# Recurrence, first sequence: rounding the weights and taking their residuals two heads ahead, at the end of a step

## What is computed

```python
q = silu(causal_dwconv(xn @ Wq, qconv_w, qconv_b))     # 4 taps along the tokens
k = silu(causal_dwconv(xn @ Wk, kconv_w, kconv_b))
q, k = layernorm over each head's 128 channels, with weight and bias
v = xn @ Wv
beta = sigmoid(xn @ Wb + bb)
def step(S, inp):                                       # one token, per sequence and head
    S = (1.0 - b) * S + b * (v_t[..., :, None] * k_t[..., None, :])
    o_t = jnp.einsum('bhvk,bhk->bhv', S, q_t)
o = o * silu(xn @ Wg);  return o @ Wo
```

## Time and profile before

| what | value |
|---|---|
| the profiled execution | 2600.33 us, span 2598.5 us |
| median of three runs | 2605.1 us |
| PE busy over the span | 2456.1 us (95%) |
| DVE, ACT, POOL busy | 1904.5, 1241.8, 849.1 us |
| mean granted clock of PE | 0.977 of full speed |
| recurrence | about 100 to 1815 us of the span |
| its first sequence | about 100 to 550 us |

### The profile page before, as it was taken

The page is one execution under the profiler, slowest core; times in us unless marked ns, Lnnn a source line. Parts: engine busy times, 40 slices in busy tenths (PEclk is TensorE's granted clock), DMA queues, the critical chain, the costliest instruction groups (busy, mean ns, idle before and its releaser), DMA issues. The chain is left out here.

```text
span 2598.5 us, 43686 instructions
## 1 busy us (share of the span) xinstructions
PE 2456.1 (95%) x14784; PEld 2175.3 (84%) x14784; DVE 1904.5 (73%) x3396; ACT 1241.8 (48%) x2025; POOL 849.1 (33%) x442
## 2 busy tenths in 40 slices
PE   4889989989999999999999999996999998999997
PEld 4778878889999989999989999996788887888886
DVE  5589999989999999999999999998422123432232
ACT  5455455545555656555555555554533223322221
POOL 1245544433434343443434343444000000221220
PEclk9999999999999999999999999998999999999999
DMA  7566566576655675666676656664551102431320
GB/s 283 166 212 212 194 221 221 201 263 205 215 195 211 210 274 195 211 218 205 210 249 231 200 204 210 211 208 142 180 204 49 65 32 73 151 121 45 113 90 23
DMA packets 242375, 462.74 MB, mean 178 GB/s; under 512 B 59382, under 2 KB 162038, under 8 KB 221178
## 3 DMA queue, kind: packets, MB, share of 16 engines
q10 hardware_dynamic: 107648, 244.34, 27.3%
q1 hardware_dynamic: 125946, 192.21, 22.0%
q0 software_dynamic: 8704, 25.19, 3.1%
HBM read 371.99 MB, written 98.07 MB: 181 GB/s over the span
## 5 line engine op out<-in xcount | busy, mean ns | idle before, releaser
L1023 DVE SCALAR_TENSOR_TENSOR xn_rows<-ps_proj,conv,xn_rows 128x1021 f32<-128x1021 f32 x381 | 486.8, 1278 | 11.6 <-ACT xn_rows L900 2.5
L1221 PE MATMUL ps_proj<-xt_hi,w_hi 128*128 128x512 f32 x1008 | 409.0, 406 | 20.1 <-DMA xt_lo<-scratch_xt_lo 12.0
L1223 PE MATMUL ps_proj<-xt_hi,w_lo 128*128 128x512 f32 x1008 | 398.5, 395 | 0.0
L1222 PE MATMUL ps_proj<-xt_lo,w_hi 128*128 128x512 f32 x1008 | 397.1, 394 | 0.0
L784 POOL TENSOR_TENSOR rc_k_state<-rc_tok_k,k_norm_rows 128x1024 f32<-128x1024 f32 x64 | 153.6, 2400 | 599.6 <-DVE rc_q_silu L1035 511.9
L1243 PE MATMUL ps_proj<-wv_hi,xt_hi 128*128 128x256 f32 x1024 | 295.2, 288 | 0.7 <-PEq L75 0.7
L1244 PE MATMUL ps_proj<-wv_lo,xt_hi 128*128 128x256 f32 x1024 | 289.8, 283 | 0.0
L1245 PE MATMUL ps_proj<-wv_hi,xt_lo 128*128 128x256 f32 x1024 | 289.8, 283 | 0.0
L1221 PEld LDWEIGHTS ps_proj<-xt_hi,w_hi 128*128 128x128 f32 x1008 | 191.9, 190 | 59.1 <-DMA xt_lo<-scratch_xt_lo 13.3
L1653 DVE TENSOR_TENSOR ff_wide_lo<-ff_wide,ff_wide_hi 128x512 fp32r<-128x512 f32 x64 | 44.4, 693 | 248.7 <-ACT ff_wide_hi L1568 248.7
L1223 PEld LDWEIGHTS ps_proj<-xt_hi,w_lo 128*128 128x128 f32 x1008 | 191.4, 190 | 42.0
(11 more groups left out here) (181 smaller groups left out, 5757.0 us busy)
## 6 DMA issues: line engine op xcount, KB each, us to landing
rc_q_rows<-scratch_rows ACTq DMA_DIRECT2D x64, 1024.0 KB, 5.1
rc_k_rows<-scratch_rows ACTq DMA_DIRECT2D x64, 1024.0 KB, 4.6
rc_decay_all<-scratch_decay ACTq DMA_DIRECT2D x64, 512.0 KB, 5.4
rc_cum_all<-scratch_cum ACTq DMA_DIRECT2D x64, 512.0 KB, 3.7
scratch_o<-rc_o_sb ACTq DMA_DIRECT2D x64, 512.0 KB, 3.5
w_hi<-scratch_w_split SPq DMA_DIRECT2D x48, 512.0 KB, 4.7
w_lo<-scratch_w_split SPq DMA_DIRECT2D x48, 512.0 KB, 5.5
wv_hi<-scratch_wv_split SPq DMA_DIRECT2D x24, 512.0 KB, 3.9
```

The source lines that it names most:

```text
L1023: nc.vector.scalar_tensor_tensor(out=act_cm[j][:, back:], in0=projected[:, 0:L - back], scalar=conv[par][:, j, t:t + 1], in1=act_cm[j][:, ...
L1221: nc.tensor.matmul(out, hi, xt_hi[:, k, cols], start=k == 0, stop=False)
L1222: nc.tensor.matmul(out, hi, xt_lo[:, k, cols], start=False, stop=False)
L1223: last = nc.tensor.matmul(out, lo, xt_hi[:, k, cols], start=False, stop=k == KC - 1)
```

## The change

ACT and POOL, in the first sequence only. `w_hi` and `w_lo` are made for the head after next (lag -2 instead of -1). On ACT `w_hi` moves from mid-step to behind the DMA of `cum`, ahead of `store_rows`. On POOL `w_lo` moves behind the power function. The v weights of the next pair are split at the end of odd steps instead of in even ones: `wv_hi` behind the row store inside `store_rows`, ahead of the normalising of k's tokens; `wv_lo` behind `w_lo`. In step 0 head 1 is split at the start, and head 2 at the end. No instruction is added or removed. The waits keep their form with other indices: the pair of heads i+2 waits for the k projection of head i, which used the same buffers.

```diff
 # POOL, step(u, par, split)
+                if first_done(A_.i):
+                    w_residual(At(u, par, -1))
                 if C_.live:
...
-                if par == 0 and split and not (isinstance(u, int) and u == 0):
-                    after_step(pool, "wv_hi_done", u)
-                    after_step(pool, "v_projected", A_.i - 1)
-                    after_pair(pool, wv_stored, u - 1, CACHED)
-                    nc.gpsimd.tensor_tensor(wv_lo[:], wv_raw[:], wv_hi[:].bitcast(F32), ALU.subtract
-                                            ).then_inc(S["wv_lo_done"], 1)
...
-                if splits(nxt.i, split):
-                    after_step(pool, "w_hi_done", nxt.i)
-                    after_step(pool, "k_projected", nxt.i - 2)
-                    nc.gpsimd.tensor_tensor(w_lo[nxt.par][:], w_raw[nxt.par][:], w_hi[nxt.par][:].bitcast(F32),
-                                            ALU.subtract).then_inc(S["w_lo_done"], 1)
...
                     nc.gpsimd.tensor_tensor(rstd_shift[:, :, 0], small[:, 5], minus_half[:], ALU.pow
                                             ).then_inc(S["rstd_done"], 1)
+                if splits(ahead.i, split):
+                    w_residual(ahead)
+                    if par == 1:
+                        after_step(pool, "wv_hi_done", u + 1)
+                        after_step(pool, "v_projected", A_.i)
+                        after_pair(pool, wv_stored, u, CACHED)
+                        nc.gpsimd.tensor_tensor(wv_lo[:], wv_raw[:], wv_hi[:].bitcast(F32), ALU.subtract
+                                                ).then_inc(S["wv_lo_done"], 1)
 # ACT, step(u, par, odd, split)
+                if first_done(A_.i):
+                    w_rounded(At(u, par, -1, odd))
                 if B_.live:
                     silu(0)
...
                     decayed_state()
                     load_cum(C_.par, C_.i, C_.pair)
+                if splits(ahead.i, split):
+                    w_rounded(ahead)
                 if B_.live:
                     store_rows()
+                if par == 1 and splits(ahead.i, split):
+                    after_pair(act, wv_loaded, u + 1)
+                    after_step(act, "v_projected", A_.i)
+                    after_pair(act, wv_stored, u, CACHED)
+                    nc.scalar.activation(wv_hi[:], wv_raw[:], ACT.Copy).then_inc(S["wv_hi_done"], 1)
+                if B_.live:
                     after_step(act, "rstd_done", B_.i)
```

More of the change, by code:

```diff
@@ L776, in step, with w_residual @@
             def step(u, par, split):
-                A_, B_, C_, D_, nxt = (At(u, par, lag) for lag in (0, LAG_B, LAG_C, LAG_D, -1))
+                A_, B_, C_, D_, ahead = (At(u, par, lag) for lag in (0, LAG_B, LAG_C, LAG_D, -2))
+                def w_residual(head):
+                    after_step(pool, "w_hi_done", head.i)
+                    after_step(pool, "k_projected", head.i - 2)
+                    after_pair(pool, w_stored[head.par], head.pair - 1, CACHED)
+                    stand(pool, keep["carrier_pool"])
+                    nc.gpsimd.tensor_tensor(w_lo[head.par][:], w_raw[head.par][:], w_hi[head.par][:].bitcast(F32),
+                                            ALU.subtract).then_inc(S["w_lo_done"], 1)
+                if first_done(A_.i):
+                    w_residual(At(u, par, -1))
                 if C_.live:
@@ L785, in step @@
                                             ALU.mult).then_inc(S["k_weighted"], 1)
-                if par == 0 and split and not (isinstance(u, int) and u == 0):
-                    after_step(pool, "wv_hi_done", u)
-                    after_step(pool, "v_projected", A_.i - 1)
-                    after_pair(pool, wv_stored, u - 1, CACHED)
-                    stand(pool, keep["carrier_pool"])
-                    nc.gpsimd.tensor_tensor(wv_lo[:], wv_raw[:], wv_hi[:].bitcast(F32), ALU.subtract
-                                            ).then_inc(S["wv_lo_done"], 1)
                 if D_.live:
@@ L800, in step @@
                                             ).then_inc(S["q_cum_done"], 1)
-                if splits(nxt.i, split):
-                    after_step(pool, "w_hi_done", nxt.i)
-                    after_step(pool, "k_projected", nxt.i - 2)
-                    after_pair(pool, w_stored[nxt.par], nxt.pair - 1, CACHED)
-                    stand(pool, keep["carrier_pool"])
-                    nc.gpsimd.tensor_tensor(w_lo[nxt.par][:], w_raw[nxt.par][:], w_hi[nxt.par][:].bitcast(F32),
-                                            ALU.subtract).then_inc(S["w_lo_done"], 1)
                 if C_.live:
@@ L873, in step @@
             def step(u, par, odd, split):
-                A_, B_, C_, D_, nxt = (At(u, par, lag, odd) for lag in (0, LAG_B, LAG_C, LAG_D, -1))
+                A_, B_, C_, D_, ahead = (At(u, par, lag, odd) for lag in (0, LAG_B, LAG_C, LAG_D, -2))
                 past = At(u, par, LAG_D + 1, odd)
@@ L942, in silu, with w_rounded @@
                                          ).then_inc(S[n + "_silu"], 1)
+                def w_rounded(head):
+                    after_pair(act, w_loaded[head.par], head.pair, 16 * W_PARTS)
+                    after_step(act, "k_projected", head.i - 2)
+                    after_pair(act, w_stored[head.par], head.pair - 1, CACHED)
+                    nc.scalar.activation(w_hi[head.par][:], w_raw[head.par][:], ACT.Copy).then_inc(S["w_hi_done"], 1)
+                if first_done(A_.i):
+                    w_rounded(At(u, par, -1, odd))
                 if B_.live:
@@ L949, in step @@
                     silu(1)
[L950 to L955, removed]
                 if A_.live and not first_done(A_.i):
@@ L962, in step @@
                     load_decay(B_.par, B_.i, B_.pair)
[L963 to L968, removed]
                 if B_.live:
```

## The result

The changed kernel takes 2580.55 us (median of 4 runs, 2578.52 to 2583.82) against 2604.01 us (2599.21 to 2606.36) before: ratio 0.9913, 95% interval 0.9894 to 0.9932. The forecast was 2575.0, its range 2559 to 2592. Its profiled execution took 2578.9 us, span 2577.1, 21.4 less than the span before. Lines have moved by 12: L1304 is now L1316, the shift L1070 is L1082, the small operations L1056 to L1058 are L1068 to L1070, the scalings L1033 and L1035 are L1045 and L1047, `w_lo` is L785, `wv_lo` L823.

What follows compares the result with a forecast made beforehand. DVE, held by POOL's SBUF reads, was taken to bound the first sequence. -47.4 + 12 + 11.4 - 2.6 = -26.6 us on the profiled 2600.3 gave 2573.7, put at 2575; range 2559 to 2592.

Steps and rivals of the forecast that it cites:

- What bounds the sequence: First sequence: DVE, held inside two-input instructions while POOL reads SBUF; 14 steps 47.4 us over PE's 25.29 each.
- Rival (d): First sequence: PE's gaps have another cause than the holds; gain about equals step 0's cost, 2600 us; chance 0.07.
- Part 1: 14 steps of the first sequence: residuals leave the stretch before the power function, saving 47.4 us at best.
- rival (b): Every step: `w_lo` meets the k scaling, three residuals per pair hold DVE 2.25 us each; 2612 us, chance 0.10.
- Part 2: Every step: `w_lo` behind the power function starts just past the shift, covered by the taps, costing nothing.
- Part 3: Ends of steps 3 to 13, odd: `wv_lo` holds the k scaling 2.1 us a pair, 12 us in all.
- two cases: k scaling: first, L1033 held 1.7 to 2.3 us; second, it starts first, `wv_lo` waits, then holds L1035 about 2.35.
- (a): Ends of odd steps: GpSimd gives way, `wv_lo` waits for the k scaling, Part 3 about 0; 2561 us, chance 0.16.
- (c): `wv_hi` delays the load of q's rows, L1033 of q waits 2.2 us more per pair; 2588 us, chance 0.11.
- Part 4: Step 0: both silus of head 0 wait behind head 2's `w_hi`, costing 11.4 us (9.5 to 13) once.
- Part 5: Change to the second sequence: entered with DVE less late, saving 2.6 us (0 to 5.3).
- the two sums of the table: Change over all stretches of the kernel: predicted -26.7 us (-26.6 in the prediction's own rounding), measured -21.4 us.

Runs made afterwards that it cites:

- Experiment 5: Kernel before with only `w_lo` moved, behind the power function in the same step: 2599.49 us in one run, the 14 steps 396.4 us.
- Experiment 3: Changed kernel without GpSimd's subtraction that makes `wv_lo` (only its semaphore counted up): 2564.47 us in one run, the 12 steps 303.54 us.
- experiment 2: As Experiment 1, and GpSimd waits for VectorE's shift to end before `w_lo`: 2568.48 us, ratio 0.987.
- experiment 7: Kernel before with both residuals replaced by short zero fills of the same tiles at the same places: 2582.61 us in one run, the 14 steps 380.1 us.
- Experiment 1: Changed kernel with head 2 alone split one step later, in step 1, at its old places: 2575.94 us, ratio 0.9887.
- experiment 8: As experiment 2, with ScalarE's two copies one place earlier and `wv_lo` in halves, the second behind VectorE's ranking: 2561.54 us, ratio 0.982.
- 6: As Experiment 5, and GpSimd waits for VectorE's shift to end before `w_lo`: 2587.70 us in one run, the 14 steps 377.9 us.
- experiment 4: Changed kernel without ScalarE's copy that makes `wv_hi` (only its semaphore counted up): 2573.70 us, the 12 steps 311.0 us.

## Why the prediction was nearly right, step by step

- **What bounds the sequence: right.** DVE's holds, not the late power function as such. Experiment 5 shows it best: `w_lo` out of the power function's way, the hold moved onto the shift, 5.1 of 47.4 us gained. Experiment 3 shows what the prediction took for the floor: 25.29 us a step with no hold left. Rival (d) is out.
- **Part 1, the 47.4 us: 2.9 of them were no hold.** The first two steps took 53.48 us before, 53.44 in experiment 2 without a held shift there, and 53.43 in experiment 7 without a residual. PE waits 3.7 us for `xn_rows` in each of the two, in both kernels. I had multiplied 14 steps by 25.29 without asking whether the first two, with a pipeline not yet full, can reach it. And the holder was misread, without harm to the sum. The prediction puts the holds down to the residuals ("three residuals per pair", rival (b)). But L1057 at 350.53 and L1058 at 380.75 start with the k addition L811. POOL, kernel before:

```profile
350.51 2.40 POOL L811 TENSOR_TENSOR rc_k_state<-rc_k_state,k_norm_rows 128x1024 f32<-128x1024 f32 x1
380.75 2.39 POOL L811 TENSOR_TENSOR rc_k_state<-rc_k_state,k_norm_rows 128x1024 f32<-128x1024 f32 x1
```

  Of the 18 small operations held by more than 0.25 us in the 14 steps of its trace, 12 lie beside L811 (25.8 of 39.3 us held) and 6 beside `w_lo`; `wv_lo` lies beside the taps and holds none. The residuals cost so much because they push the k addition to where the small operations start; with them out of the way it is through in time, and both kinds of hold go.
- **Part 2, `w_lo` at no cost: right for 12 steps, wrong for the two before.** With a fourth head in flight `w_lo` starts 0.7 to 1.1 us behind the shift (245.46 and 246.25; the row at 246.25 above) and runs beside the taps. Before that the `cum` load has no states to wait for and doesn't keep `w_hi` back, `w_lo` meets the shift, and this is rival (b)'s mechanism, twice: 4.1 us in experiment 2, of which 2.0 lie ahead of the first L1316. The argument against (b), "L870 hangs on D's states", has no D in these steps.
- **Part 3, the k scaling held by `wv_lo`: right.** It was put at 2.1 us a pair, and L1047 lasts 2.1 us longer than L1045 does (3.30 against 1.21). Of its two cases the second came in five pairs, the first in the sixth. The six pairs cost 10.2 us over PE's time instead of 12, shown by experiment 3. Of (a) nothing is left; `wv_lo` too is lengthened, but lets only one scaling pass. Nor did DVE wait for q's rows (c): no such wait of note is in the 12 steps of the changed kernel.
- **Part 4, step 0: the chain right and put 1.0 us too high, a held shift of 2.2 us left out.** ACT, then PE, in the changed kernel:

```profile
117.51 1.06 ACT L955 ACTIVATE w_hi<-raw 128x1024 fp32r<-128x1024 f32 x1 [15.24 <-DMA raw<-in_wk]
118.58 1.28 ACT L947 ACT_TABLE_LOAD   x1
119.88 1.06 ACT L947 ACTIVATE rc_q_silu<-xn_rows 128x1024 f32<-128x1024 f32 x1
```

```profile
120.99 1.97 PE L1209 MATMUL rc_ps_work<-ident,rc_q_silu 128*128 128x128 f32 x8 [8.80 <-ACT rc_q_silu L947]
122.61 0.78 PE L1233 MATMUL ps_proj<-xt_hi,w_hi 128*128 128x512 f32 x1
123.18 0.63 PE L1234 MATMUL ps_proj<-xt_lo,w_hi 128*128 128x512 f32 x1
```

  The chain is the one that the prediction worked out for the earlier trace rows, but the raw weights came at 117.5, not 120.4, so the turn of q is 8.4 us later than its 112.63, not 11.3. PE had been idle since 112.2, and behind the gap it runs slower: a matmul takes 0.63 us, where it took 0.39 before the gap (at 111.80), and the granted clock from 116.70 to 127.00 is 0.50, the level of 1.2 GHz. Experiment 1 gives 10.4 us for all this, where the prediction had 11.4; the held shift adds 2.0 to 2.2, which the sum had not. That the two errors leave only 1.2 us is luck.
- **Part 5, the change of sequence: wrong.** It fell by 0.5, not 2.6. PE waits there for the second sequence's `xt_lo`, 7.0 us before and 6.8 after; SP issues that load 1.5 us behind the start of L1304 before and 1.2 behind L1316 after (531.34 and 509.97), since it overwrites a tile that the last v projection reads. The load lands 12.0 us after its issue, with the 16 DMA engines busy throughout (share 1.06 from 509.97 to 521.96). How late DVE is plays no part: in experiment 8, where the last two steps take 25.29 and 25.45 us, the change still takes 35.17. PE's wait after, then SP's issues:

```profile
PE ps_proj L1233 <- DMA xt_lo<-scratch_xt_lo: 6.8, 1, 6.8
```

```profile
509.07 0.80 SPq L734 DMA_DIRECT2D xt_hi<-scratch_xt_hi  x1
509.97 1.21 SPq L734 DMA_DIRECT2D xt_lo<-scratch_xt_lo  x1
```

  In experiment 3 this wait is 3.6 us and the change 30.78; the load lands 9.0 us after its issue there, with the DMA engines as busy (1.07), and why stays open.

Together: 1.2 too little in step 0, 4.2 in the first two steps and 2.1 at the change of sequence, less 1.8 too much in the pairs, less 0.6 that lies ahead of the recurrence; that is 5.1 of the 5.3 us between the two sums of the table, and the other 0.2 lie behind the change of sequence.

## What to carry to other kernels

When an instruction of VectorE lasts ten times as long as its twin elsewhere, look at what GpSimd runs at that moment; it can be work that others have pushed there, as the k addition here. When GpSimd's work is moved, list every two-input operation of VectorE that it will lie beside in each kind of step, those of a pipeline still filling too: the hold moves with it. A place beside operations that read one tile in SBUF cost nothing here (taps of 3.91 us), a wait on GpSimd for the short operation to pass can pay (18.5 us in the 14 steps between experiments 5 and 6), and halving what can't be placed lessens what it holds (7.0 us between 2 and 8). Before a step's excess is booked as gain, ask for each stretch what else sets its length.

## What the runs showed of the hardware

Who is held is decided by order, and it goes back and forth within one meeting: `wv_lo`, 0.2 us behind the start of L1045, waited and took 3.26 us; L1047, issued while it ran, took 3.30. Where `wv_lo` came first it took its own time and L1045 waited: 2.38 and 2.67 us in experiment 4, 2.39 and 3.30 in the sixth pair of the changed kernel. The prediction read the same two durations in the earlier trace rows as both engines being held at once. This is the rule of the Trainium skill ("SBUF — State Buffer", section "Who interferes with whom"): the order of issue decides which of the two blocks, for the whole instruction. The trace agrees, and adds that an instruction in the middle of a queue of the other engine's instructions lets just one pass. None of this waiting is shown as idle time: it stands inside the durations.
